# Last pass of a four-layer graph network: the share product of one of four node columns goes from VectorE to ScalarE, and VectorE's two operations are split by PSUM bank

## What is computed

```python
# last layer, cut
h = (x @ W.T).reshape(N, H, C)                 # H = 4 heads, C = 64
p = exp(leaky_relu(a_s[src] + a_d[dst]) - m[dst])   # edges and one loop per node
alpha = p / (denom[dst] + 1e-16)
out = segment_sum(alpha[:, :, None] * h[src], dst)  # N x 256
out = elu(out + bias) + x
x = layernorm(x + out)
```

## Time and profile before

| what | value |
|---|---|
| median of 3 runs | 5101.81 us (5099.42 to 5104.55) |
| the profiled execution: its own time | 5100.59 us |
| the profiled execution: span from first to last instruction | 5098.9 us |
| mean granted TensorE clock over the span | 0.912 |
| last pass, from its first transpose to the end of the span | 4543.7 to 5098.9 us |
| busy share of the span: PE, DVE, ACT, POOL | 82%, 69%, 38%, 63% |

### The profile page before, as it was taken

One profiled execution on the slowest core, in us unless ns is written; L12 is line 12 of the kernel. 1 busy time (PEld: TensorE's weight loads), 2 busy tenths in 40 slices (PEclk: granted clock), 3 DMA queues, 4 the chain that ended last, 5 costly groups with the idle time before them and its releaser, 6 DMA issues. The chain is left out here.

```text
span 5098.9 us, 69926 instructions
## 1 busy us (share of the span) xinstructions
PE 4199.0 (82%) x18336; PEld 3042.4 (60%) x18336; DVE 3509.5 (69%) x10200; ACT 1961.3 (38%) x3445; POOL 3218.7 (63%) x3078
## 2 busy tenths in 40 slices
PE   2177759998999999999999999766676687768886
PEld 1055535555666666666666666555566576767675
DVE  3055546666666666666666666599999688879998
ACT  0011115553333333333333333344444222237776
POOL 7388754444456666666566665677776677757776
PEclk6589879999999999999999999888877788889999
DMA  9988879998544444444444444255554444448886
GB/s 374 324 157 154 161 140 361 364 367 318 192 172 155 143 141 139 139 144 143 142 143 149 148 147 141 101 182 182 191 187 171 132 138 138 139 165 297 296 296 229
DMA packets 449380, 994.26 MB, mean 195 GB/s; under 512 B 147560, under 2 KB 230474, under 8 KB 449198
## 3 DMA queue, kind: packets, MB, share of 16 engines
q1 hardware_dynamic: 296146, 732.73, 42.3%
q0 software_dynamic: 100736, 172.47, 13.6%
q10 hardware_dynamic: 52316, 87.06, 5.1%
HBM read 493.48 MB, written 541.33 MB: 203 GB/s over the span
## 5 line engine op out<-in xcount | busy, mean ns | idle before, releaser
L1140 PE MATMUL psum<-W2b,arena 128*128 128x256 f32 x3136 | 725.2, 379 | 0.0
L1121 PE MATMUL psum<-arena,W1b 128*128 128x512 f32 x1568 | 699.1, 599 | 0.0
L1140 PEld LDWEIGHTS psum<-W2b,arena 128*128 128x128 f32 x3136 | 573.1, 190 | 66.3 <-issue 0.5
L1121 PEld LDWEIGHTS psum<-arena,W1b 128*128 128x128 f32 x1568 | 289.8, 190 | 402.8 <-issue 402.8
L1009 ACT ACTIVATE arena<-psum,hbias 128x512 f32<-128x512 f32 x392 | 269.5, 688 | 559.2 <-PE psum L1121 559.2
L825 DVE TENSOR_SCALAR arena<-arena 128x256 f32<-128x256 f32 x392 | 135.2, 408 | 439.2 <-POOL arena L820 439.2
L1367 PE MATMUL psum<-Wg,arena 128*128 128x264 f32 x784 | 275.6, 485 | 195.4 <-ACT arena L1402 183.8
L959 POOL DMA_INDIRECT xd_d<-arena,FE x360 | 356.7, 991 | 99.3 <-issue 99.3
L464 POOL DMA_INDIRECT tab<-arena x196 | 311.3, 1588 | 167.0 <-DMA tab<-zero 67.8
L816 POOL TENSOR_TENSOR arena<-arena,lneps 128x4 f32<-128x4 f32 x196 | 41.9, 214 | 553.1 <-DVE arena L812 552.3
L603 PE MATMUL psum<-arena,NEG 128*128 128x324 f32 x500 | 178.2, 523 | 247.6 <-ACT arena L409 214.9
(11 more groups left out here) (349 smaller groups left out, 10141.8 us busy)
## 6 DMA issues: line engine op xcount, KB each, us to landing
arena<-in_x SPq DMA_DIRECT2D x194, 512.0 KB, 5.6
x_d<-arena SPq DMA_DIRECT2D x194, 512.0 KB, 3.6
tab<-zero SPq DMA_DIRECT2D x11, 5832.0 KB, 55.1
arena<-x_d SPq DMA_DIRECT2D x105, 512.0 KB, 4.7
tab<-blank SPq DMA_DIRECT2D x97, 544.0 KB
arena<-tab SPq DMA_DIRECT2D x97, 544.0 KB, 5.3
h_d<-arena SPq DMA_DIRECT2D x98, 512.0 KB, 4.7
arena<-h_d SPq DMA_DIRECT2D x98, 512.0 KB
```

The costliest lines, as they stand in the source:

```text
L1121: last = pe.matmul(psum[:, HB[c], :], W1b[:, f, c * P:(c + 1) * P], x1T[:, f, :], start=False, stop=(f == FH - 1))
L1140: last = pe.matmul(outB(j), hid[:, c, j * P:(j + 1) * P], W2b[:, c, :], start=(c == 0), stop=(c == KH - 1))
```

## The change

In `l_scalar` a new function `share(k)` stands first in the body of step k. It waits for `mm(k)` and the table rows and multiplies column 3 of the step's matmul output by its shares in place in PSUM: four activations of 64 elements, one for each head, each with the share as its scale operand (one number for each partition). The last of them raises the new semaphore `pa`.

In `l_vector` the product and the addition of 1024 elements each become four operations: the product of columns 0 and 1 (512 elements, first bank), the addition for columns 0 and 1 (512), then a wait for `pa`, the product of column 2 (256, second bank), the addition for columns 2 and 3 (512). Each addition still waits for the product before it. `t` is raised by both additions, so all that wait for it count two to a step; the waits mean the same as before.

```diff
             def mm(k):
-                wait(pe, lp["t"], k.s - 1)
+                wait(pe, lp["t"], 2 * k.s - 2)
...
+            def share(k):
+                wait(act, lp["mm"], k.s + 1)
+                wait(act, l_t[k.slot(NTT)], 16 * (k.turn(NTT) + 1))
+                for h in range(H3):
+                    f = slice((J - 1) % 2 * D + h * HD3, (J - 1) % 2 * D + (h + 1) * HD3)
+                    done = act.activation(psum[:, 3 + 2 * k.slot(2), f], psum[:, 3 + 2 * k.slot(2), f], ACT.Copy,
+                                          scale=l_tt[:, k.slot(NTT), J - 1, WC3 + h:WC3 + h + 1])
+                done.then_inc(lp["pa"].sem, 1)
...
             def body(k):
+                share(k)
                 if live(k.plus(2), NS):
                     evac(k.plus(2))
                 exps(k)
...
                 wait(v, lp["mm"], k.s + 1)
                 wait(v, l_t[k.slot(NTT)], 16 * (k.turn(NTT) + 1))
-                v.tensor_tensor(out=own..., in0=own..., in1=l_tt[..., WC3:WC3 + H3]..., op=ALU.mult).then_inc(lp["pr"].sem, 1)
-                wait(v, lp["pr"], k.s + 1)
-                v.tensor_tensor(out=l_sum[:, b, :, :], in0=own..., in1=l_tt[:, k.slot(NTT), :, 0:D],
-                                op=ALU.add).then_inc(lp["t"].sem, 1)
+                v.tensor_tensor(out=mine[:, 0:2, :, :], in0=mine[:, 0:2, :, :], in1=share[:, 0:2, :, :].to_broadcast([P, 2, H3, HD3]),
+                                op=ALU.mult).then_inc(lp["pr"].sem, 1)
+                wait(v, lp["pr"], 2 * k.s + 1)
+                v.tensor_tensor(out=l_sum[:, b, 0:2, :], in0=rows[:, 0:2, :], in1=l_tt[:, k.slot(NTT), 0:2, 0:D], op=ALU.add).then_inc(lp["t"].sem, 1)
+                wait(v, lp["pa"], k.s + 1)
+                v.tensor_tensor(out=mine[:, 2:3, :, :], in0=mine[:, 2:3, :, :], in1=share[:, 2:3, :, :].to_broadcast([P, 1, H3, HD3]),
+                                op=ALU.mult).then_inc(lp["pr"].sem, 1)
+                wait(v, lp["pr"], 2 * k.s + 2)
+                v.tensor_tensor(out=l_sum[:, b, 2:4, :], in0=rows[:, 2:4, :], in1=l_tt[:, k.slot(NTT), 2:4, 0:D], op=ALU.add).then_inc(lp["t"].sem, 1)
```

More of the change, by code:

```diff
@@ L1980, in gnn_program @@
                   rs=e2["rs"].after(CS + 1), nm=e2["nm"].after(CS + 1), y=e2["y"].after(J * CS))
-        lp.update({k: Signal(sem(f"l_{k}")) for k in ("pr", "t")})
+        lp.update({k: Signal(sem(f"l_{k}")) for k in ("pr", "t", "pa")})
         l_t = [e3_gd[b].after(16 * turns(b)) for b in range(NG)]
@@ L1993, in tables @@
                 b = k.slot(NTT)
-                wait(sp, lp["t"], k.s - NTT + 1)
+                wait(sp, lp["t"], 2 * (k.s - NTT + 1))
                 a, n = node_view(tab, k)
@@ L2041, in evac @@
                     act.activation(l_xT[:, k.slot(2), f, :], l_tr[:, f, :], ACT.Copy).then_inc(lp["xT"].sem, 1)
+            def share(k):
[6 more added lines that the diff above has]
+                done.then_inc(lp["pa"].sem, 1)
             def exps(k):
-                wait(act, lp["t"], k.s + 1)
+                wait(act, lp["t"], 2 * k.s + 2)
                 wait(act, lp["u"], k.s)
@@ L2111, in weighted @@
                 own = psum[:, c:c + 2, :]
+                share = l_tt[:, k.slot(NTT), :, WC3:WC3 + H3].rearrange("p j (h a) -> p j h a", a=1)
+                mine = own.rearrange("p a (j h c) -> p (a j) h c", j=2, h=H3)
+                rows = own.rearrange("p a (j d) -> p (a j) d", j=2)
                 wait(v, lp["mm"], k.s + 1)
                 wait(v, l_t[k.slot(NTT)], 16 * (k.turn(NTT) + 1))
-                v.tensor_tensor(out=own.rearrange("p a (j h c) -> p (a j) h c", j=2, h=H3), in0=own.rearrange("p a (j h c) -> p (a j) h c", j=2, h=H3),
-                                in1=l_tt[:, k.slot(NTT), :, WC3:WC3 + H3].rearrange("p j (h a) -> p j h a", a=1).to_broadcast([P, J, H3, HD3]),
+                v.tensor_tensor(out=mine[:, 0:2, :, :], in0=mine[:, 0:2, :, :], in1=share[:, 0:2, :, :].to_broadcast([P, 2, H3, HD3]),
                                 op=ALU.mult).then_inc(lp["pr"].sem, 1)
-                wait(v, lp["pr"], k.s + 1)
-                v.tensor_tensor(out=l_sum[:, b, :, :], in0=own.rearrange("p a (j d) -> p (a j) d", j=2), in1=l_tt[:, k.slot(NTT), :, 0:D],
-                                op=ALU.add).then_inc(lp["t"].sem, 1)
+                wait(v, lp["pr"], 2 * k.s + 1)
[5 more added lines that the diff above has]
+                v.tensor_tensor(out=l_sum[:, b, 2:4, :], in0=rows[:, 2:4, :], in1=l_tt[:, k.slot(NTT), 2:4, 0:D], op=ALU.add).then_inc(lp["t"].sem, 1)
             def unit(k):
```

## The result

The changed kernel takes 5475.93 us (median of 3 runs, 5474.93 to 5476.49), against 5101.81: a ratio of 1.0735, interval 1.0716 to 1.0754. That is 374 us more. The prediction was 5502, with a range of 5450 to 5560, and slower with a chance of 0.95. The direction and the mechanism held; the amount was 26 us too high.

What follows compares the result with a forecast made beforehand. VectorE bounds the kernel at 5.40 us a step; the new wait makes it 9.62. 95 rounds add 400.9 us, less 0.2 at the end: 5501 for the profiled execution, 5502 us for the median, range 5450 to 5560.

Steps and rivals of the forecast that it cites:

- The loop: Share to next share, through VectorE, GpSimd's residual and rstd, and ScalarE's normed: one round each step, 9.62 us.
- today's way round: Kernel before, back to VectorE through ScalarE's exponential: 9.48 us over two steps, 4.74 a step, hidden under 5.40.
- From U's start to ScalarE's next body: VectorE's U, GpSimd's residual and small operations, then ScalarE's normed: 7.42 us of the round.
- Product of column 2 to the addition: VectorE's second product of 256 elements to its second addition, start to start: 0.45 us of the round.
- Addition to U: VectorE's second addition to its operation U, start to start: 0.60 us of the round.
- mis-sized term is share: ScalarE's four activations: 1.10 us, bounds 0.57 and 1.58, plus 0.05 from pa to VectorE's product.
- The remark in the prediction: On ScalarE's share: copies out of PSUM look slightly cheaper, so 1.10 us was taken where the sum was 1.12.
- The sum: Last pass: 95 rounds at 9.62 in place of 5.40 us, +400.9; -0.2 after the last share; 5502 us.
- VectorE's saving: VectorE's list: 0.27 us of elements saved against two more instructions, 0.03 us a step shorter, 3 us in all.
- Hidden at 5099 us: Rival: ScalarE's part is hidden and VectorE's list stays the bound, no change, 5099 us; chance 0.03.
- A faster kernel at 5075 us: Rival: VectorE gets the whole saving of 26 us with ScalarE's part hidden, 5075 us, faster by 0.5%; chance 0.02.
- TensorE's clock: TensorE: if its clock falls, eight transposes take 1.97 us, a step some 8.5 us, still under 9.62.

Runs made afterwards that it cites:

- work without the wait: Changed kernel with ScalarE's four activations on a constant tile, VectorE not waiting for them, column 3's product left out: 5119.4 us, ratio 1.0036.
- share a step ahead: Changed kernel with the share of step k+1 in ScalarE's body k, behind the copies and ahead of the exponential: 5098.46 us, ratio 0.9997.
- normed a step later: Changed kernel with normed(k-3) and store(k-4) in ScalarE's body k, in place of normed(k-2) and store(k-3): 5176.3 us, ratio 1.0147.
- The four on a constant tile: Changed kernel with four more activations of the same size, on a constant tile into a spare one, before share's own four: 5565.54 us, ratio 1.0913.
- the merged version with normed later: Changed kernel with share one step ahead, VectorE's four operations merged to two, ScalarE's normed and store one step later: 5079.48 us, ratio 0.9957.

## Why the prediction was right

**The loop.** Right, and shown: work without the wait, share a step ahead and normed a step later each take out one link of it and leave the others. The last two land where the remaining loops were computed to put them; the first came out 18 us above its expected 5101, by a loop of three steps that was found only afterwards and then tested. That today's way round goes over two steps and is hidden, and the new one over one step, was the step on which all hung.

**Its length, term by term.** From U's start to ScalarE's next body: 7.42 predicted, 4813.37 - 4805.97 = 7.40 measured. Product of column 2 to the addition: 0.45 and 0.47. Addition to U: 0.60 and 0.61. The **mis-sized term is share**: 1.10 and 0.05 for the wait were predicted, 4804.89 - 4804.00 = 0.89 for both was measured. The source view of share's line (lengths in ns: least, median, most) says why:

```profile
L2048 ACT ACTIVATE psum<-psum,arena x392: 254/267/295, 4550.7 to 5451.9; 128x64 f32<-128x64 f32 x196
```

An activation takes 267 ns with its scale operand, where 350 was summed from a 64-element row and an operand's price. The row had its size, but its input and output lie in SBUF. The four on a constant tile, SBUF to SBUF, took 1.05 us, close to the 1.10; so the sum was good for that case, and it is PSUM to PSUM that is cheaper. Rows of the kernel before speak for a part of both ends, source and destination (1024 elements each: from SBUF to SBUF; from SBUF to PSUM with an operand; from PSUM to SBUF):

```profile
L1419 ACT ACTIVATE arena<-arena 128x1024 f32<-128x1024 f32 x49 | 51.8, 1056 | 1.5
L2047 ACT ACTIVATE psum<-arena,minus 128x1024 f32<-128x1024 f32 x98 | 108.4, 1106 | 4.1 <-DVE arena L2125 3.5 <-DVE arena L2118 0.6
L1447 ACT ACTIVATE arena<-psum 128x1024 f32<-128x1024 f32 x1 | 1.0, 1002 | 0.0
```

With the operand's 91 ns taken off, writing to PSUM saves 1056 + 91 - 1106 = 41 ns, and reading from it 1056 - 1002 = 54 ns (a single instruction). These are estimates, from other sizes and functions; their sum of 95 is somewhat above the 347 - 267 = 80 that share shows. The remark in the prediction that copies out of PSUM look slightly cheaper pointed the right way, but took off 0.02 where it should have taken 0.26.

**The sum.** The timeline has share of step 2 and of the last step, and the U after it, at:

```profile
4559.80 0.88 ACT L2048 ACTIVATE psum<-psum,arena 128x64 f32<-128x64 f32 x4
...
5451.33 0.87 ACT L2048 ACTIVATE psum<-psum,arena 128x64 f32<-128x64 f32 x4
...
5453.30 1.22 DVE L2141 SCALAR_TENSOR_TENSOR arena<-psum,arena 128x1024 f32<-128x1024 f32 x1
```

(5451.33 - 4559.80) / 95 = 9.38 us a step, so the 95 rounds take 891.53 us in place of 513.03, +378.5. The start is 2.2 us earlier than W(2) in the earlier trace rows: in this execution the phases ahead were done sooner, with the pass's first transposes at 4540.2 us (source view of their line, below) where the earlier trace rows have 4543.73. The last share to U is 1.97 us, where W to U was 2.39: -0.4. Together +375.9, which is the difference of the spans, 5474.8 - 5098.9. The prediction's +400.9 is some 22 us above the +378.5 measured (95 x (9.62 - 9.38)), all of it from share. The other 4 of the 26 us lie outside the loop: 2.2 are the earlier start, and 1.8 the place of the median beside the profiled execution (5476.49 us, 0.6 above the median here; 1.2 below it before).

```profile
L2016 PE MATMUL psum<-ident,arena x784: 272/332/477, 4540.2 to 5426.8; 128*128 128x128 f32 x196
```

**VectorE's saving.** Predicted as 0.03 us a step, close to none; share one step ahead, which runs VectorE's new list without the loop, is 0.9997 of before. The forecast that the change is worthless even where share is hidden is shown.

**The rivals.** Hidden at 5099 us: the run with share one step ahead has that time (5098.46; the interval of its ratio is some 5 us either way), and the rival's condition is what that run supplies; in the changed kernel the order of ScalarE's list forbids it. The Trainium skill, PSUM — Partial Sum Buffer, section Specifications (TRN2), has ScalarE and VectorE using PSUM in parallel at full bandwidth when they don't meet in a bank. That run agrees, with a product of 0.68 us beside a share of 0.88; the rule was not what decided the changed kernel's time. A faster kernel at 5075 us: the merged version with normed later is at 5079.48, but needs three more edits than the change had.

**TensorE's clock.** The stretches above have a granted clock of 0.81 to 0.86, a mix of the two levels of 1.2 and 2.4 GHz, where the earlier trace rows have 1.00. In the step shown TensorE had waited 4.83 us for the copies; its transposes then took 1.97 and its matmuls 5.61, from 4805.91 to 4813.29 or 7.4 us, under the 9.37 of a round, and the share that follows still starts right behind normed: TensorE is off the loop, as the prediction had it.

## What to carry to other kernels

When a piece of work goes to an engine that has idle time, don't compare the work with the idle time: write down the loop that its result closes, link by link through each engine's list, and count over how many steps it goes. A loop over two steps that is hidden becomes the bound when a new wait lets it close in one; moving the new piece one step ahead opened it again at no cost (0.9997), and moving the piece behind which it stands one step back gave back 300 of the 374 us, up to the next loop of one step. It pays to write down that next loop too: in three of the runs it set the time. And splitting an operation to make room for a second engine has its own price: here two more instructions were worth as much as the elements that went.

## What the hardware showed that was not expected

Four activations of 64 elements with a scale operand took 0.86 us from PSUM to PSUM in place and 1.05 us from SBUF to SBUF, in the same run and one behind the other. By the rows of the kernel before shown above, source and destination each have a part in it, by estimate some 54 and 41 ns an instruction; no run moves only one of the two ends of share.

Work on an engine that is 90% busy or more cost nothing or some 17 us by its place alone: the same four activations of 0.95 us a step gave 5119.4 us ahead of the copies and 5099.72 behind them.
